# Attention denominators: one diagonal block moves from a ones-matmul to a GpSimd addition

## The reference, cut to what matters

```python
x = x + layernorm(attention(layernorm(x)))      # 32 heads of 32, 8 key/value heads, rope, causal softmax
x = x + layernorm(ffn(layernorm(x)))            # 1024x1024 base product + top-2 of 8 rank-16 adapters
# inside attention, of each head:
scores = where(causal, q @ k.T / sqrt(32), -1e20)
out = softmax(scores) @ v                       # the divisor: sum over the keys of exp(scores - shift)
```

## Time and profile before

| | us |
|---|---|
| three runs | 1065.66, 1067.73, 1068.37; median 1067.73 |
| the profiled execution: its own time | 1066.51 |
| its span, first to last instruction | 1064.5 |
| TensorE busy | 1017.9 (96% of the span) |
| VectorE, ScalarE, GpSimd busy | 636.3, 399.5, 411.5 |
| mean granted TensorE clock | 0.983 of 2.4 GHz |

### The profile page before, as it was taken

How to read it: one execution, slowest core, us unless ns; L and a number is a source line. 1 busy time by engine, 2 the same in 40 slices (tenths; PEclk the granted TensorE clock), 3 DMA queues, 4 the chain that set the end, 5 groups by cost and what they waited for, 6 DMA issues and landing times.

```text
span 1064.5 us, 17672 instructions
## 1 busy us (share of the span) xinstructions
PE 1017.9 (96%) x6614; PEld 829.7 (78%) x6614; DVE 636.3 (60%) x1882; ACT 399.5 (38%) x682; POOL 411.5 (39%) x461
## 2 busy tenths in 40 slices
PE   4999999999989998999999989899999999999995
PEld 3888888898876665666666558799999999999995
DVE  7354443424447886878788636566666666666654
ACT  7132221210127775777777733222222222222221
POOL 1072552433337775777776730111122211111110
PEclk8999999999999998999999999899999999999999
DMA  9144332237237776556555344222222222222101
GB/s 354 51 158 139 119 135 103 79 124 183 96 122 193 205 197 167 144 135 159 141 137 146 114 146 137 72 89 80 79 80 79 79 81 86 82 86 86 58 20 40
DMA packets 78788, 127.31 MB, mean 120 GB/s; under 512 B 7792, under 2 KB 47088, under 8 KB 75632
## 3 DMA queue, kind: packets, MB, share of 16 engines
q1 hardware_dynamic: 78704, 126.19, 39.2%
HBM read 85.27 MB, written 40.37 MB: 118 GB/s over the span
## 4 chain that ended last, share of the span: by engine, by line
PE 88%; DVE 4%; DMA 2%; POOL 2%; ACT 2%; issue 1%; SPq 0%; POOLq 0%; DVEq 0%; ACTq 0%
PE bank L1237 19%; PE bank L1238 19%; PE bank L1239 19%; PE bank L1310 8%; PE bank L1336 7%; PE bank L1350 7%; PE bank L1367 5%; PE bank L1446 1%; DVE ln_st L928 1%; PE bank L1246 1%; DMA q_t<-shift_l 1%; DMA den_i<-inv_scratch 1%; POOL turn L656 1%; POOL turn L659 1%; DVE xt_l L945 1%
## 5 line engine op out<-in xcount | busy, mean ns | idle before, releaser
L990 DVE CUSTOM_DVE_ANT_0 bank<-bank,row_mask 128x128 f32<-128x128 f32 (+1 forms) x480 | 219.3, 523 | 62.3 <-PE bank L1310 59.0
L642 POOL TENSOR_TENSOR ln_rs<-ln_ve,minus_half 128x1 f32<-128x1 f32 x64 | 61.5, 961 | 412.2 <-DVE ln_mm L933 412.2
L815 ACT ACTIVATE prob<-bank 128x512 f32<-128x512 f32 x320 | 172.7, 599 | 38.2 <-PE bank L1336 38.0
L1237 PE MATMUL bank<-xt_h,wq_h 128*128 128x512 f32 x320 | 128.0, 400 | 4.5 <-DVE wq_l L953 4.5
L1237 PE MATMUL bank<-wf_h,xt_h 128*128 128x384 f32 (+1 forms) x384 | 129.8, 338 | 1.8 <-DVE z L1148 1.8
L1239 PE MATMUL bank<-wf_l,xt_h 128*128 128x384 f32 (+1 forms) x384 | 130.2, 339 | 0.0
L1238 PE MATMUL bank<-wf_h,xt_l 128*128 128x384 f32 (+1 forms) x384 | 130.1, 339 | 0.0
L1310 PE MATMUL bank<-k_t,q_t 96*128 96x384 f32 (+3 forms) x512 | 124.7, 340 | 2.6 <-DVE row_top L990 2.6
L1239 PE MATMUL bank<-xt_l,wq_h 128*128 128x512 f32 x320 | 125.8, 393 | 0.0
L1238 PE MATMUL bank<-xt_h,wq_l 128*128 128x512 f32 x320 | 125.8, 393 | 0.0
L1336 PE MATMUL bank<-q_t,k_t 98*128 98x512 f32 x320 | 111.4, 415 | 6.4 <-DMA q_t<-shift_l 3.1
(11 more groups left out here) (108 smaller groups left out, 1898.6 us busy)
## 6 DMA issues: line engine op xcount, KB each, us to landing
q_t<-q_scratch SPq DMA_DIRECT2D x32, 512.0 KB, 5.2
q_scratch<-turn_h SPq DMA_DIRECT2D x16, 512.0 KB, 2.7
q_scratch<-turn SPq DMA_DIRECT2D x16, 512.0 KB, 3.0
q_t<-q_scratch SPq DMA_DIRECT2D x32, 256.0 KB, 5.5
att_scratch<-att SPq DMA_DIRECT2D x32, 256.0 KB, 2.9
at_raw<-att_scratch SPq DMA_DIRECT2D x16, 512.0 KB, 3.9
x<-x SPq DMA_DIRECT2D x16, 512.0 KB, 4.3
out<-z SPq DMA_DIRECT2D x15, 512.0 KB, 2.9
```

The lines of the kernel that those rows point to most:

```text
L642: nc.gpsimd.tensor_tensor(ln_rs[j][:], ln_ve[j][:], minus_half[:], ALU.pow).then_inc(count, 1)
L815: nc.scalar.activation(prob[n % 2][:, i, :, :].rearrange("p h q -> p (h q)"), bank[3 + (NS * n + i) % 3][:], ACT.Exp, scale=INV_SQRT_HD).t ...
L990: last = nc.vector.tensor_tensor_reduce(out=row, in0=row, in1=row_mask[:, SEQ - w:SEQ], scale=1.0, scalar=LOWEST, op0=ALU.add, op1=ALU.max ...
L1237: mm(dst, a_h, w_h, start=start, stop=False, skip_group_check=True)
```

## The change

GpSimd adds a fourth time per group: `add_keys(n, 3)` puts the masked diagonal block 2 (block 7) onto half 0 of `key_sum`, between add 2 and mask 3. Its waits are for mask 2 and add 0 of the same group, and for the exponential of block 7. `SUMS` = 4 replaces the count 3 in the semaphore values. D becomes three runs of two blocks for each head: blocks 0 and 1, the two halves of `key_sum`, and diagonals 1 and 3, which now go in one run to query blocks 1 and 3 of the bank (`dst[:, 1:4:2, :]`). All else stands.

```diff
--- before.py
+++ after.py
@@ -50,6 +50,7 @@
 NR = len(ROWS)
 SCORES = [(kc, qb) for kc in range(TT) for qb in range(kc, TT)]
 NS = len(SCORES)
+SUMS = 4
 FIRST = [SCORES.index((kc, kc)) for kc in range(TT)]
 FFN_ORDER = (6, 0, 1, 4, 2, 3, 5, 7)
 SPILL = 256
@@ -686,10 +687,12 @@
             def add_keys(n, i, total, a, b):
 
                 pool.wait_ge(prob_ready, NS * n + b + 1)
+                if i == 3:
+                    pool.wait_ge(prob_masked, TT * n + 3)
                 if i < 2:
                     wait(pool, den_ps, n - 1)
                 else:
-                    pool.wait_ge(prob_summed, 3 * n + 2)
+                    pool.wait_ge(prob_summed, SUMS * n + (1 if i == 3 else 2))
                 first = total if a is None else prob[n % 2][:, a, :, :]
                 nc.gpsimd.tensor_tensor(total, first, prob[n % 2][:, b, :, :], ALU.add).then_inc(prob_summed, 1)
 
@@ -708,6 +711,7 @@
                 add_keys(n, 1, total[:, 1, :, :], SCORES.index((0, 3)), SCORES.index((1, 3)))
                 mask(n, 2)
                 add_keys(n, 2, total[:, 1, :, :], None, SCORES.index((2, 3)))
+                add_keys(n, 3, total[:, 0, :, :], None, FIRST[2])
                 mask(n, 3)
                 if 1 <= n <= NPIECE:
                     piece_lo(n - 1)
@@ -1356,16 +1360,19 @@
             def denominators(n):
 
                 pe.wait_ge(prob_masked, TT * n + TT)
-                pe.wait_ge(prob_summed, 3 * n + 3)
+                pe.wait_ge(prob_summed, SUMS * n + SUMS)
                 pe.wait_ge(att_ready, n + 1)
                 p, total = prob[n % 2], key_sum[n % 2]
-                for i in range(4):
-                    for h in range(REP):
-                        what, at, w = ((p[:, 0:2, h, :], 0, 2), (total[:, :, h, :], 2, 2),
-                                       (p[:, FIRST[1]:FIRST[1] + 1, h, :], 1, 1),
-                                       (p[:, FIRST[2]:FIRST[3] + 1:2, h, :], 2, 2))[i]
-                        last = mm(bank[6][HD * h:HD * h + HD, P * at:P * (at + w)].rearrange("p (b q) -> p b q", q=P),
-                                  ones[:], what, start=(i == 0), stop=(i == 3), skip_group_check=True)
+                for h in range(REP):
+                    dst = bank[6][HD * h:HD * h + HD, :].rearrange("p (b q) -> p b q", q=P)
+                    mm(dst[:, 0:2, :], ones[:], p[:, 0:2, h, :], start=True, stop=False, skip_group_check=True)
+                for h in range(REP):
+                    dst = bank[6][HD * h:HD * h + HD, :].rearrange("p (b q) -> p b q", q=P)
+                    mm(dst[:, 2:4, :], ones[:], total[:, :, h, :], start=False, stop=False, skip_group_check=True)
+                for h in range(REP):
+                    dst = bank[6][HD * h:HD * h + HD, :].rearrange("p (b q) -> p b q", q=P)
+                    last = mm(dst[:, 1:4:2, :], ones[:], p[:, FIRST[1]:FIRST[3] + 1:FIRST[3] - FIRST[1], h, :],
+                              start=False, stop=True, skip_group_check=True)
                 last.then_inc(den_ps, 1)
 
             pe.wait_ge(ident_loaded, 16)
```

## The result

The changed kernel is slower. Its median is 1081.05 us (1079.72 to 1084.96, six runs) against 1067.68 us before (1065.66 to 1068.74), a ratio of 1.0137 with a 95% interval of 1.0116 to 1.0159. The prediction was 1085.8 us in a range of 1077 to 1092.

What follows compares the result with a forecast made beforehand. TensorE's gapless matmul chain bounds the kernel, with a thin margin before V3. 1066.51 + 0.69 + 24.84 + 1.24 - 6.09 - 0.21 - 0.46 - 0.71 gives 1085.8 us, range 1077 to 1092.

Steps and rivals of the forecast that it cites:

- What bounds the kernel: One attention step was 9.39 us, a chain of waits of TensorE alone, all matmul work without a gap.
- the margin: Mask 3 ends at 517.67 and V3 loads weights at 518.00: a third of a microsecond, against an addition of 1.24.
- The stall and the loop: V3 waits for the late mask 3; nothing gives it back, the loop repeats, and steps grow from 9.39 to 10.10 us.
- the term of 0.92: V3's stall in each common step, 518.95 against 518.03; 27 steps of steps 2 to 29 give +24.84 us.
- V3's place: V3 follows nine blocks of V, 1.92 us after V's start: 518.24 in the common step, 518.03 with the shorter D.
- Two signs that came out otherwise: Expected in the profile: a wait of about 0.9 us before V3, and a chain passing over `copy_sums` and exponential 6.
- allows nearly the same: Before add 1 on GpSimd: D sets its start through exponential 6, and add 0 permits nearly the same start.
- D's saving: D loses one block and gives 0.21 us a step: -6.09 us over steps 1 to 29.
- Step 30 and the end: Step 30 takes the whole addition, +1.24 us; D gives -0.21 in step 31 and -0.46 in step 32.
- Step 1: V3 of step 1 streams at 323.92 instead of 323.23, as D had not yet run: +0.69 us.
- The term of -0.71: Step 10's wait for the shift's DMA shrinks because the shift is needed 0.71 us later; ends 0 and 5.4.
- The third rival, the clock: New stalls lower TensorE's clock in each step, about 2.3 us in each of 28, giving 1150 us; chance 4%.

Runs made afterwards that it cites:

- Experiments 1 and 2: Changed kernel with add 3 moved behind mask 3: 1060.57 us; changed kernel with mask 3 ahead of both add 2 and add 3: 1060.36 us.
- experiments 8 and 9: Changed kernel with the third-diagonal addition cut from four heads to two: 1069.27 us; cut to one head: 1063.05 us.
- experiment 4: Changed kernel with the old D of seven blocks, keeping the fourth addition ahead of mask 3: 1091.75 us.
- experiments 1 to 3: Experiments 1 and 2, and the changed kernel without the fourth addition, leaving the new D alone: 1061.05 us.
- experiment 6: Changed kernel with the two bias-row loads moved from step 8 to steps 12 and 14: 1079.85 us.
- experiment 5: Kernel before the change with the two bias-row loads moved from step 8 to steps 12 and 14: 1062.83 us.

## Why the prediction was right, and what it mis-sized

**What bounds the kernel, and the margin.** Right. The kernel before was TensorE's work without a gap, and the number that decided was the third of a microsecond between mask 3 and V3. Experiments 1 and 2 show it directly: the order of two GpSimd instructions is worth 20 us.

**The stall and the loop.** Right in mechanism: a wait before V3 released by the mask in every step but step 10 (29 waits), steps of 10.04 us where 10.10 were forecast, nothing given back. The stall is 10.04 - 9.18 = 0.86 us, so the term of 0.92 was 0.06 too long in each step. It counted 0.25 us from the end of the mask to V3's streaming, where the changed kernel shows V3 starting after 0.15, and it set V3's place from block counts. Together they put the margin at 0.32; experiments 8 and 9 measure 0.38. Over 27 steps that is 1.8 us. Another 0.5 us went because steps 4, 5 and 12 of the kernel before had small delays of 0.08 to 0.25 us that the longer steps hide.

**Two signs that came out otherwise.** The wait in the trace is 0.65 us and not about 0.9. The recorded end of the matmuls ahead of it (514.43 us, the start of V in that step, + 2.14) lies 0.22 us behind V3's place by block counts (514.43 + 1.92), so the stall is read from the step and not from the wait. And the chain of waits does not pass over `copy_sums` and exponential 6. That is the way it takes in experiment 4; in the changed kernel the way over exponential 5 and add 0 is as long, which the prediction had as "allows nearly the same".

**D's saving.** Right: D takes 1.43 us in the chains of experiments 1 to 3, 0.22 less than before, against 0.21.

**Step 30 and the end.** +1.01 against +1.03 for step 30, -0.62 against -0.67 behind it. The second agreement is in part luck: step 31 alone lies anywhere from 16.5 to 18.5 us in the profiled executions. D's saving shows in step 32, with 16.21 to 16.23 us in all kernels with the old D and 16.01 or 16.02 in all with the new one.

**Step 1.** +1.75 against +0.69. V3 of step 1 does wait for the mask in the changed kernel, 0.49 us, and does not in experiment 6. The kernels without a stall lie anywhere from 323.67 to 325.51 us at this point, so the size of the term can't be read from one pair of executions.

**Step 10.** The term of -0.71 was mis-sized: -4.38 with D's part, against -0.92. The wait shrank by 0.94, to 2.15, and in this execution the clock held, which saved another 3.2. In two others of the same kernel the wait was 2.93 and 2.94 and the clock fell; there the step was only 1.0 and 2.0 us shorter than in the kernel before. The prediction had the whole as an end of its range and took the near end as the value. That far end was itself too small. It was put at 5.4, from a mean clock of 0.77 between 410 and 420 us, but the low clock had begun at the end of the wait, at 407.8. The whole is 15.99 - 9.39 = 6.6 us, and experiment 5 took it all from step 10.

**How good the forecast was.** It was 4.7 us too high against the profiled execution. The stall's term accounts for 2.3 of that, step 10 for 3.5, and step 1 went the other way by 1.1. Where the clock falls in step 10, the kernel takes 1084 to 1085 us and the forecast of 1085.8 looks closer than its terms were. That is luck.

**The third rival, the clock.** It did not happen. The granted clock between 325 and 622 us is full in the profiled execution, in spite of 29 waits of 0.4 to 1.0 us before V3. The Trainium skill ("TensorE: Matmul & The Clock Gate", section "HAM oscillation — how this bites in real kernels") warns of loops whose waits send the array back to half clock in each turn; the waits of its example are of 3 to 5 us, several times those here. In this trace waits of 0.65 us in steps of 10 never did it. Single waits of 2.93 and 2.94 us in other executions of the same kernel did.

**A rule to read with care.** The Trainium skill ("Perfetto Trace Analysis", section "Identifying the Most-Contended Engine") takes the engine with the highest occupancy as the one to optimize first. For TensorE it asks for the kernel's share of peak rate and for the weight loads' busy share, in place of the matmuls'. By busy time of matmuls or of weight loads that engine is TensorE here (96% and 78%, GpSimd 39%). The change did just that: TensorE's busy time fell by 2.8 us in the page and its weight loads' by 9. The kernel lost 13, because the work went ahead of a result of GpSimd that TensorE needed 0.33 us after it was ready.

## What to carry to other kernels

Before work is moved to an engine with idle time, read when that engine's next urgent result is due, and put the new work behind it, not ahead. A wait that shows nothing in a profile may have a margin of a few tenths of a microsecond, and only start and end times side by side show it. Where a loop over several engines takes over, the step becomes that loop's length, and the timelines of its engines are enough to add it up to 0.1 us.

## What the hardware did that was not expected

The length of a wait of 2 to 3 us does not tell what TensorE's clock does after it. In the profiled execution of 1080.83 us the granted clock stayed at 2.4 GHz after the 2.15 us in step 10. In step 30 of the same execution TensorE waited 2.14 us, ran one product and waited another 0.47; in this second wait the clock fell to 1.2 GHz, for 3.4 us. Ten of the traces have the wait for the shift's DMA ahead of step 10's last products, with 2.15 to 3.55 us. The clock fell in nine of them, after 2.38 us in experiment 4 too, and held only after the 2.15. The wait itself came out at 2.15, 2.93 and 2.94 us in three executions of the one kernel.

Nor does it fall at a fixed place. With 1084.03 us it fell inside the wait of 2.93 us and came back 5.5 us after its end. With 1084.39 us and a wait of 2.94 it fell 1.4 us after the end and was low for 3.3 us, so that the six small products still took 0.85 us and V took 3.79. What decides between these is open. For the price it is enough to know that such a wait can cost more than its length: from the execution with 2.93 us to the one with 2.15 the wait is 0.78 us shorter and step 10 is 3.4 us shorter.
